# Up projection of the second layer's feed-forward part: two float32 products per tile against six float32r products of split operands

## What is computed

```
n  = layernorm(x3_in) * ln_gamma + ln_beta             # (4096, 256)
W1 = (fc1_q - 128) * fc1_scales                        # (256, 1024), scale per 128 rows
h  = silu(n @ W1 + fc1_bias)                           # the up projection
y  = h @ W2 + fc2_bias                                 # W2 likewise; down projection
```

## Time and profile before

| what | value |
|---|---|
| time, median of 3 runs | 1133.39 us (1132.06 to 1133.58) |
| the profiled execution's own time | 1132.27 us |
| its span, first to last instruction | 1130.5 us |
| mean granted PE clock over the span | 0.967 of full |
| busy: PE, PEld | 1023.1 us (91%), 701.0 us (62%) |
| busy: DVE, ACT, POOL | 922.9 us (82%), 841.1 us (74%), 701.5 us (62%) |
| chain that ended last, by engine | PE 18%, ACT 9%, DVE 8%, issue 5%, POOL 3% |
| up projection on PE, 7 blocks (L40 bank_m<-oa,w) | 103.2 us in 224 MATMULs |

### The profile page before, as it was taken

The page is one execution under the profiler, slowest core; times in us unless marked ns, Lnnn a source line. Parts: engine busy times, 40 slices in busy tenths (PEclk is TensorE's granted clock), DMA queues, the critical chain, the costliest instruction groups (busy, mean ns, idle before and its releaser), DMA issues. The chain is left out here.

```text
span 1130.5 us, 17117 instructions
## 1 busy us (share of the span) xinstructions
PE 1023.1 (91%) x5234; PEld 701.0 (62%) x5234; DVE 922.9 (82%) x1166; ACT 841.1 (74%) x1641; POOL 701.5 (62%) x623
## 2 busy tenths in 40 slices
PE   5999999999969999998758699999999999988987
PEld 4777777777744344444536367567676766767576
DVE  7899999999843566545899998999999899999741
ACT  7778877887644455556767888898998989896843
POOL 2466666766751444435766968869697886968420
PEclk9999999999989999999778899999999999999999
DMA  6344434442404011114976576557566675755201
GB/s 195 113 131 129 129 99 136 121 134 82 137 26 163 1 37 38 38 53 102 240 152 165 127 166 131 151 131 172 139 146 167 142 162 139 151 137 133 81 1 37
DMA packets 93230, 133.81 MB, mean 118 GB/s; under 512 B 8786, under 2 KB 47698, under 8 KB 93140
## 3 DMA queue, kind: packets, MB, share of 16 engines
q1 hardware_dynamic: 93140, 132.73, 44.5%
HBM read 116.45 MB, written 14.16 MB: 116 GB/s over the span
## 5 line engine op out<-in xcount | busy, mean ns | idle before, releaser
L2219 DVE TENSOR_TENSOR_SCAN oa<-bank_a,h,oa 128x512 f32<-128x512 f32 x128 | 159.7, 1270 | 13.7 <-ACT h L1896 10.8
L2219 DVE TENSOR_TENSOR_SCAN ob<-bank_a,h,ob 128x512 f32<-128x512 f32 x128 | 160.5, 1269 | 9.4 <-ACT bank_a L1887 7.0
L1714 PE MATMUL bank_m<-w,f_h 128*128 128x256 f32 x448 | 104.7, 384 | 0.0
L40 PE MATMUL bank_m<-oa,w 128*128 128x512 f32 x224 | 103.2, 595 | 1.2 <-ACT oa L1954 0.9
L1887 ACT ACTIVATE bank_a<-dtc,A 128x512 f32<-128x512 f32 x128 | 86.7, 683 | 16.0 <-DVE oa L2219 8.6
L1887 ACT ACTIVATE bank_a<-s,A 128x512 f32<-128x512 f32 x128 | 86.4, 682 | 15.3 <-DVE oa L2219 9.2
L1714 PEld LDWEIGHTS bank_m<-w,f_h 128*128 128x128 f32 x448 | 84.8, 193 | 13.1 <-issue 2.4
L1669 PE MATMUL bank_y<-ident,ob 128*128 128x128 f32 x512 | 71.5, 286 | 19.9 <-DVE ob L2225 19.9
L1892 ACT ACTIVATE bank_c<-Cb 128x512 f32<-128x512 f32 x128 | 75.5, 590 | 17.3 <-DVE ob L2225 13.2
L2428 POOL TENSOR_TENSOR oa<-uc,Bb 128x1024 f32<-128x1024 f32 x32 | 75.7, 2366 | 20.4 <-DVE ob L2225 13.4
L1669 PEld LDWEIGHTS bank_y<-ident,ob 128*128 128x128 f32 x512 | 63.0, 148 | 39.7 <-DVE ob L2225 22.6
(11 more groups left out here) (374 smaller groups left out, 2735.0 us busy)
## 6 DMA issues: line engine op xcount, KB each, us to landing
Bb<-CB_rows SPq DMA_DIRECT2D x128, 256.0 KB, 5.0
Cb<-CB_rows SPq DMA_DIRECT2D x128, 256.0 KB, 4.6
abc<-decays SPq DMA_DIRECT2D x32, 512.0 KB, 4.4
Ebc<-ramps SPq DMA_DIRECT2D x64, 128.0 KB, 3.0
uT<-in_uT SPq DMA_DIRECT2D x8, 512.0 KB, 4.6
u<-in_u SPq DMA_DIRECT2D x8, 512.0 KB, 3.9
x_tokens<-x2s SPq DMA_DIRECT2D x8, 512.0 KB, 2.9
x_rows<-x1T SPq DMA_DIRECT2D x8, 512.0 KB, 2.8
```

The lines of the kernel that those rows point to most:

```text
L40: i = e.matmul(out, w, x, start=(n == 0), stop=(n == len(pairs) - 1))
L1714: i = e.matmul(to, f_h[:, k, c * CH:(c + 1) * CH], w2[:, k, :], start=False, stop=(c % 2 == 1 and k == KF - 1))
L2219: e.tensor_tensor_scan(s[:, k, :], p_a[k][:, :], s[:, k, :], h0[:, n, k:k + 1], ALU.mult, ALU.add).then_inc(v_s, 1)
```

## The change

- `w1` becomes two float32r tiles, `w1_h` (rounded) and `w1_l` (the remainder). The integer codes are loaded into two tiles that are idle then; `weights(6)` makes the float32 product in place of `s1`, `weights(8)` rounds it, and a new `weights(15)` subtracts.
- `evac_normed` reads its PSUM bank twice on ACT: once into `nT_h` (float32r), once into `nT` (float32) as before. `end_normed` likewise, in halves.
- POOL makes `nT_l = nT - nT_h` in `low_normed`, between `into 13` and `drive`; in the last block DVE does so in `end_low`.
- `up_proj` and `end_up` sum six float32r passes, and the first of each block waits for the remainder.
- The semaphores of constants in the first layer are merged (`a_W`, `a_negA`, `a_id`, `a_rate` into `a_const`; `v_init`, `v_negA`, `v_W` into `v_const`; `p_Wo` into `p_const`), and `v_q` into `v_m`, with counts adapted; the order of instructions stays.

```diff
-        w1, w2 = sb("w1", [P, KD, FF]), sb("w2", [P, KF, DM])
+        w1_h, w1_l = (sb(n, [P, KD, FF], F32R) for n in ("w1_h", "w1_l"))
+        w2 = sb("w2", [P, KF, DM])
...
-            loaded += [(w1[:, :, :].bitcast(I32), rows(d["f_q1"])), (w2[:, :, :].bitcast(I32), rows(d["f_q2"]))]
+            q1 = [flat(dtc[0]).bitcast(I32), flat(uc[0]).bitcast(I32)]
+            loaded += [(q1[k], rows(d["f_q1"])[:, k, :]) for k in range(KD)] + [(w2[:, :, :].bitcast(I32), rows(d["f_q2"]))]
...
                     if w == 6:
                         e.wait_ge(ld, DMAS * len(loaded))
-                        e.tensor_scalar(w1[:, :, :], w1[:, :, :].bitcast(I32), -128.0, None, ALU.add).then_inc(c_w, 1)
+                        for k in range(KD):
+                            e.scalar_tensor_tensor(s1[:, k, :], q1[k], -128.0, s1[:, k, :], ALU.add, ALU.mult).then_inc(c_w, 1)
...
-                        e.tensor_tensor(w1[:, :, :], w1[:, :, :], s1, ALU.mult).then_inc(c_w, 1)
+                        e.tensor_copy(w1_h[:, :, :], s1).then_inc(c_w, 1)
...
+                    if w == 15:
+                        e.wait_ge(c_w, 5)
+                        e.tensor_tensor(w1_l[:, :, :], s1, w1_h[:, :, :].bitcast(F32), ALU.subtract).then_inc(c_w, 1)
...
                 def up_proj(b, m):
                     if m == 0:
-                        e.wait_ge(a_ft, 2 * b + 2)
+                        e.wait_ge(a_ft, 4 * b + 4)
+                        e.wait_ge(p_nl, b + 1)
                     elif m > 1:
                         e.wait_ge(a_up, 8 * b + m - 1)
-                    passes(e, pair[m % 2][:, :], [(w1[:, k, m * P:(m + 1) * P], nT[:, k, :]) for k in range(KD)]).then_inc(pe_up, 1)
+                    ws = slice(m * P, (m + 1) * P)
+                    passes(e, pair[m % 2][:, :], [(w[:, k, ws], x[:, k, :]) for w, x in ((w1_h, nT_h), (w1_l, nT_h), (w1_h, nT_l)) for k in range(KD)]).then_inc(pe_up, 1)
...
                 def end_up(p, m):
                     if m == 0:
-                        e.wait_ge(a_ft, 2 * Z + 2 * p + 2)
+                        e.wait_ge(a_ft, 4 * Z + 4 * p + 4)
+                        e.wait_ge(v_nl, p + 1)
...
                 def evac_normed(b, k):
                     after(e, pe_up, 8 * b)
                     e.wait_ge(pe_ft, 2 * b + k + 1)
+                    e.activation(nT_h[:, k, :], pair[k][:, :], ACT.Identity, bias=lb[:, k:k + 1], scale=lg[:, k:k + 1]).then_inc(a_ft, 1)
                     e.activation(nT[:, k, :], pair[k][:, :], ACT.Identity, bias=lb[:, k:k + 1], scale=lg[:, k:k + 1]).then_inc(a_ft, 1)
...
                     for k in range(KD):
-                        e.activation(nT[:, k, p * DM:(p + 1) * DM], wide[p][:, k * DM:(k + 1) * DM], ACT.Identity, bias=lb[:, k:k + 1], scale=lg[:, k:k + 1]).then_inc(a_ft, 1)
+                        for to in (nT_h, nT):
+                            e.activation(to[:, k, p * DM:(p + 1) * DM], wide[p][:, k * DM:(k + 1) * DM], ACT.Identity, bias=lb[:, k:k + 1], scale=lg[:, k:k + 1]).then_inc(a_ft, 1)
...
+                def end_low(p):
+                    ts = slice(p * DM, (p + 1) * DM)
+                    e.wait_ge(a_ft, 4 * Z + 4 * p + 4)
+                    e.tensor_tensor(nT_l[:, :, ts], nT[:, :, ts], nT_h[:, :, ts].bitcast(F32), ALU.subtract).then_inc(v_nl, 1)
...
                 second(Y, 1)
+                end_low(0)
                 stats6(Y, 1)
+                end_low(1)
...
+                def low_normed(b):
+                    e.wait_ge(a_ft, 4 * b + 4)
+                    e.sem_inc(step, 1)
+                    e.tensor_tensor(nT_l[:, :, :], nT[:, :, :], nT_h[:, :, :].bitcast(F32), ALU.subtract).then_inc(p_nl, 1)
...
                         into(cur, 13)
+                    if 0 <= post < NB - 1:
+                        low_normed(post)
                     if live(nxt):
                         drive(nxt)
```

More of the change, by code:

```diff
@@ L150, in first_layer @@
             ld_W = [sem(f"ld_W{part}") for part in range(3)]
-            p_const, p_Wo, a_W, a_negA, a_id, v_init, v_negA, v_W, a_rate = (sem(n) for n in (
-                "consts", "W_out", "W_h", "expA", "diag", "zeroed", "negA", "W_l", "rates"))
+            p_const, a_const, v_const = (sem(n) for n in ("consts", "a_consts", "v_consts"))
             early = [(cn_w1, rows(d["cn_w1"])), (cn_w2, rows(d["cn_w2"])),
@@ L297, in carried @@
                     e.wait_ge(a_Dx, g + 1)
-                    e.wait_ge(v_init, 4)
+                    e.wait_ge(v_const, 4)
                     after(e, a_S, g)
@@ L518, in split_W @@
                     e.wait_ge(ld_W[part], DMAS)
-                    e.activation(W_h[:, :, W_part[part]], W_in[:, :, W_part[part]], ACT.Copy).then_inc(a_W, 1)
+                    e.activation(W_h[:, :, W_part[part]], W_in[:, :, W_part[part]], ACT.Copy).then_inc(a_const, 1)
                 e.wait_ge(ld_col, DMAS)
                 e.preload_act_table_set(EXP_LN)
-                e.activation(negA[:, :], vec_at["A_log"], ACT.Exp).then_inc(a_negA, 1)
+                e.activation(negA[:, :], vec_at["A_log"], ACT.Exp).then_inc(a_const, 1)
                 e.wait_ge(p_const, 6)
@@ L526, in scalar @@
                     i = e.activation(b_id[:, c * CH:(c + 1) * CH], ident[:, :], ACT.Copy)
-                i.then_inc(a_id, 1)
-                e.wait_ge(v_init, 4)
+                i.then_inc(a_const, 1)
+                e.wait_ge(v_const, 4)
                 split_u(0)
@@ L614, in scalar @@
                     if it == 2:
-                        e.activation(A[:, :, :].rearrange("p k n -> p (k n)"), vec_at["c_A_log"], ACT.Exp).then_inc(a_rate, 1)
+                        e.activation(A[:, :, :].rearrange("p k n -> p (k n)"), vec_at["c_A_log"], ACT.Exp).then_inc(a_const, 1)
                     if live(old):
@@ L717, in low_W @@
                 def low_W(part):
-                    e.wait_ge(a_W, part + 1)
-                    e.tensor_tensor(W_l[:, :, W_part[part]], W_in[:, :, W_part[part]], W_h[:, :, W_part[part]].bitcast(F32), ALU.subtract).then_inc(v_W, 1)
+                    e.wait_ge(a_const, part + 3)
+                    e.tensor_tensor(W_l[:, :, W_part[part]], W_in[:, :, W_part[part]], W_h[:, :, W_part[part]].bitcast(F32), ALU.subtract).then_inc(v_const, 1)
                 def first_low_u():
@@ L746, in net_columns @@
                     e.tensor_scalar(hg3[:, :], gc_b3, 0.5, None, ALU.mult)
-                    e.wait_ge(a_rate, 1)
+                    e.wait_ge(a_const, 6)
                     e.tensor_scalar(A[:, :, :], A[:, :, :], -1.0, None, ALU.mult)
-                e.memset(raw[:, :, TB:TB + TAPS - 1], 0.0).then_inc(v_init, 1)
-                e.memset(S[:, :, :], 0.0).then_inc(v_init, 1)
-                e.memset(Sb[:, :, :], 0.0).then_inc(v_init, 1)
-                e.memset(zeros[:, :], 0.0).then_inc(v_init, 1)
-                e.wait_ge(a_negA, 1)
-                e.tensor_scalar(negA[:, :], negA[:, :], -1.0, None, ALU.mult).then_inc(v_negA, 1)
+                e.memset(raw[:, :, TB:TB + TAPS - 1], 0.0).then_inc(v_const, 1)
+                e.memset(S[:, :, :], 0.0).then_inc(v_const, 1)
+                e.memset(Sb[:, :, :], 0.0).then_inc(v_const, 1)
+                e.memset(zeros[:, :], 0.0).then_inc(v_const, 1)
+                e.wait_ge(a_const, 1)
+                e.tensor_scalar(negA[:, :], negA[:, :], -1.0, None, ALU.mult).then_inc(v_const, 1)
                 first_low_u()
@@ L1166, in z_first @@
                 def z_first(p):
-                    e.wait_ge(c_w, 11)
+                    e.wait_ge(c_w, 12)
                     e.wait_ge(c_xT, 11 + p)
@@ L1480, in build @@
             xl, xn, x3, x3b = (t(n, [P, NC, DM])[:, :, :] for n in ("xl", "xn", "x3", "x3b"))
-            f_h = t("f_h", [P, KF, TB])
+            f_h, nT_h = t("f_h", [P, KF, TB]), t("nT_h", [P, KD, TB], F32R)
+            nT_l = t("nT_l", [P, KD, TB], F32R)
             state, prod, gT, nT = [oa[0], ob[0], oa[1], ob[1]], [ob[2], oa[2]], ob[3], oa[3]
@@ L1500, in build @@
             turned, wide, up_at = p_a, (p_c, p_m[1]), (p_y[0], p_y[1], p_a[0], p_a[1])
-            v_e, v_b, v_m, v_q = (d_sem("v_" + n) for n in ("e", "b", "m", "q"))
+            v_e, v_b, v_m = (d_sem("v_" + n) for n in ("e", "b", "m"))
+            p_nl, v_nl = d_sem("p_nl"), d_sem("v_nl")
             half = slice(0, 2), slice(2, 4)
@@ L1749, in end_up @@
                         e.wait_ge(a_up, 8 * Z + (m | 1) + 1)
-                    ts = slice(p * DM, (p + 1) * DM)
-                    passes(e, up_at[m // 2][:, (m % 2) * DM:(m % 2 + 1) * DM], [(w1[:, k, m * P:(m + 1) * P], nT[:, k, ts]) for k in range(KD)]).then_inc(pe_up, 1)
+                    ts, ws = slice(p * DM, (p + 1) * DM), slice(m * P, (m + 1) * P)
+                    passes(e, up_at[m // 2][:, (m % 2) * DM:(m % 2 + 1) * DM], [(w[:, k, ws], x[:, k, ts]) for w, x in ((w1_h, nT_h), (w1_l, nT_h), (w1_h, nT_l)) for k in range(KD)]).then_inc(pe_up, 1)
                 def end_down(p):
```

32 lines of the change are left out of this document (16 added, 16 removed).

## The result

The changed kernel takes 1153.38 us (median of 4 runs, 1152.76 to 1154.67), the kernel before 1133.49 us in the 4 runs beside it: ratio 1.0181, with a 95% interval from 1.0165 to 1.0196. The change costs 20 us. The prediction was 1147 us, 14 more than before, with a range from 1135 to 1159.

The account below looks back on a forecast made before the run. It took a loop of DVE and ACT to set the scan stage's pace, with PE following with slack, and PE to be the path at the end. 13.0 + 1.2 + 0.4 = 14.6 us more gave 1147 us, range 1135 to 1159.

Parts of the forecast that it names:

- part 4: Last block's halves: more evacuations and end_low delay PE, 48 short passes at 0.125 us apart; 1.2 us more (0 to 11.5).
- Rival (a): Scan stage: PE sets the pace, so 15 us come back and the kernel gets faster, 1118 us; chance 10%.
- rival (b): Scan stage: ACT and DVE regain the 1.7 us in the silu burst; about +2, 1135 us; chance 7%.
- Part 1: Up projection in the scan stage: PE saves 2.1 us per block, 15 in seven, worth 0 to the kernel.
- Part 2: Two more evacuations on ACT per block in the scan stage: the instructions themselves cost 0.1 us.
- Part 3: Scan stage: POOL's remainder delays up_proj(0), then ACT, then scan(13, 0); 1.70 us per block, 13.0 in all (0 to 20).
- Part 5: Making the split weights, mainly the subtraction in weights(15), costs 0.4 us (0 to 1); merged semaphores cost 0.
- (c): Last block: short passes are bound by weight loads, 11.5 us instead of 1.2; 1157 us; chance 10%.
- (d): Scan stage: POOL's added 2.37 us operation holds up a DVE scan, 17 us on top; 1164 us; chance 4%.

Follow-up runs that it names:

- short wait: Changed kernel with add_up 10 ahead of up_proj(0), the remainder made in halves, and only the last two passes waiting, each for its half: 1138.09 us, 1.0054.
- filled float32 kernel: Changed kernel with float32 up_proj products in seven blocks, no weights' remainder, and ten identity products on PE ahead of the wait: 1155.75 us, 1.0209.
- instructions alone: Kernel before plus the second evacuation on ACT and the remainder on POOL, unread, in seven blocks; PE stays float32 and never waits for POOL: 1135.47 us, 1.0026.
- end-only: Kernel before with float32r passes in the last block alone, ordered so that the remainder is hidden: 1129.88 us against 1131.76, 0.9978.
- filled kernel: Changed kernel with twelve needless identity products on PE in each of the last block's two waits for the remainder: 1151.60 us, 1.0182.
- moved evacuation: Changed kernel with evac_up(0) moved on ACT behind carry 11, decay(13, 0) and spread_C 12: 1151.04 us, 1.0158.
- float32 products: Changed kernel with up_proj of seven blocks multiplying float32 nT by rounded weights, all waits kept: 1167.05 us, 1.0297.
- late wait: Changed kernel with up_proj(0) waiting for POOL's remainder only before its fifth pass: 1143.17 us, 1.0087.

## Why the prediction was right, and where it was short

The time lies in the range, and the chain that was forecast for the scan stage is in the trace and answers to edits of its links. The size was short, 14.6 us against 20.6, and the term that was most wrong is part 4.

**What bounds the kernel.** Right. With the wait short and PE's products shorter, the block is not shorter (67.18 against 66.98), so PE does not set the pace; that DVE and ACT do is read from the waits. Rival (a) falls with that, and rival (b) with the trace: nothing took the wait back.

**Part 1, PE's time is worth 0.** Right for the kernel before and for the short wait. Too simple for the change itself, where PE is late: there 2.1 us of products are worth 0.85 per block, by the filled float32 kernel. The sum did not suffer, since it had let the 2.1 us only make PE catch up. The passes came as priced, 0.232 to 0.235 apart.

**Part 2** gave 0.1 us per block; the instructions alone cost a steady block 0.24, POOL's among them.

**Part 3, the wait.** Right in every link, each a little short. PE waits 2.43 us for POOL (2.5 predicted), ACT 2.65 (2.5), DVE 1.69 (1.6), and the remainder ends 3.85 us after the old `nT` (3.7). Offsets from the gate of the fourth block:

| us | before | after | later by | predicted |
|---|---|---|---|---|
| up_proj(0) starts | 47.26 | 50.51 | 3.25 | 3.1 |
| evac_up(0) starts | 49.17 | 52.19 | 3.02 | 2.83 |
| decay(13, 0) starts | 50.68 | 52.87 | 2.19 | 2.02 |
| scan(13, 0) starts | 51.73 | 53.68 | 1.95 | 1.70 |

The 0.25 are small handoffs: POOL starts 0.18 us behind ACT's end (786.89 to 787.07), PE 0.15 behind POOL's, and the scan 0.81 behind the start of its decay, where I had taken 0.1, 0.1 and 0.73.

In the second block the reading was wrong, though the number (4.0 against 2.8) looks near. The 0.97 us of slack that I missed there did not cost anything: the wait before scan(13, 0) is 1.69 us as in every block. In its place DVE waits 3.46 us for `bank_c` where it had waited 1.21. The kernel with the instructions alone, which has no new wait, shows 3.49 us there; the end-only kernel, whose code in that block is that of before, shows 2.79 and took 65.82 us against 64.25. In all three ACT waits 2.8 to 2.9 us for the transposes at evac_normed(0), just ahead of spread_C 10, where it had waited 1.27, and the stretch of half clock in which they run is 10.2 us long instead of 6.8. So of the 4.0 us 1.7 are the named wait, about 0.7 the second evacuation ahead of spread_C 10 (I had taken 0.1), and about 1.6 a stretch of half clock that end-only has without any change in this block; what makes it longer stays open. The last block varies by as much: end-only took 68.55 there against 67.07. In the changed kernel PE's wait there was 4.60 us and was followed by half clock, for which the 1.7 had no term; its 2.3 can't be told from scatter.

And the prediction followed the lateness through evac_up(0) alone; moving that one showed evac_up(1) as the next that hands it on.

**Part 4, the end.** Here the prediction failed by most of its error: 4.9 us against 1.2. The two waits are as predicted (1.72 and 1.69 more, 1.7 named). The passes are 0.119 apart at full clock where I took 0.125, so 48 take 5.8 us and not 6.1; and the 32 MATMULs of before took 7.0 and 6.8 us, not 7.2, since their transposes take 0.6 us of the distance and not 0.44. The two errors cancel. The page TensorE: Matmul & The Clock Gate of the Trainium skill (section Back-to-back issue gap) has a formula for the gap of an isolated MATMUL, by which the estimate was 0.109; the trace lies between, nearer to mine, and decides. What failed is that I priced the passes at full clock behind a wait that the change itself makes. At half clock they are (1114.67 - 1113.39) / 6 = 0.213 apart. The estimate by that section's formula for the low clock, columns / 1.2 ns, is 0.213 too. The first half took 7.28 us instead of 5.8 and the second 7.09. That is 2.8 of the missing 3.7 us, by the filled kernel.

The rest is 1.15 us at the out projection. The gate came earlier against the rest, since PE had caught up: DVE waited for the last sum 1.64 us instead of the 2.79 of the earlier trace rows. But ACT's normalization beside it did not. It now waits for POOL's `nb`, which is made from DVE's statistics of `x3b`, and these stand 1.14 us closer to the gate than before. So ACT's copy to `ob` and PE's out projection (its first MATMUL, with the bias, at 1088.77) start 1.15 us later from the gate. ACT's normalization before, and DVE's gate and the same ACT row after:

```profile
1069.24 2.07 ACT L1970 ACTIVATE x3b<-x3b,nb,rs 128x256 f32<-128x256 f32 x4
```
```profile
1085.37 1.29 DVE L2243 TENSOR_TENSOR zgs<-bank_y,zgs 128x512 f32<-128x512 f32 x2 [1.64 <-PE bank_y L1676]
1086.16 2.07 ACT L1981 ACTIVATE x3b<-x3b,nb,rs 128x256 f32<-128x256 f32 x4 [1.04 <-POOL nb L2480]
```

So of the 2.1 us of shorter products that I let come back in the last scan, about half was lost again behind the gate. The filled kernel has the same 1.15 at full clock, so the half clock that happens to stand there (the 3.09 us of the first `w_o` products) cost nothing: the next ones wait for ACT anyway.

**Part 5, the weights.** Predicted 0.4. No run can tell: the first scan of the third stage starts between 535.3 and 537.7 us in the kernels with the new weights, and at 536.6 and 535.5 in the two with the old ones.

**Rivals (c) and (d).** (c) needed 0.232 per short pass; it is 0.119. (d) did not happen: the pair of scans that begins at 788.60, across the end of POOL's remainder, takes 2.45 us as before, and the instructions alone, POOL's among them, cost a steady block only 0.24 us. The rule on ports of the page SBUF — State Buffer (Trainium skill, section Who interferes with whom) agrees.

**The sum.** Predicted 13.0 + 1.2 + 0.4 = 14.6. Measured in the profiled executions, by the table of gates: 17.1 + 4.9 - 1.3 = 20.7 (20.6 as the difference of the spans, by rounding). Of the 6 us missing, 2.8 are the clock in the end, 1.2 the half clock in the fifth block, 1.1 the small excess of the other blocks from the third to the seventh, 1.15 the out projection; the second and the last block hold 1.8 that cannot be told from scatter, the stages before gave 1.7 back, which is scatter too and was luck, and 0.3 came back elsewhere in the end. Fewer busy microseconds on PE were no sign of anything: 10 less (17 predicted), with the half clock taking part of the gain.

## What to carry to other kernels

When a product is replaced by a faster one that needs one more prepared operand, follow the new operand to the first instruction that waits for it, and then every queue behind that instruction: here 2.1 us saved on an engine with slack bought 2 us lost on the engine without it. Order the passes so that those needing the late operand come last, and start preparing it in halves; that alone took back 14 of 20 us. And behind every wait that an edit adds on PE, price the next products at half clock as well as at full, and let the range hold both.

## What the runs showed of the hardware that was not expected

The granted clock behind a wait of PE. Behind 2.90 and 2.80 us of idle time in the end the products ran at half clock for 3.4 us; with identity products in the gap they did not. Without a filling, half clock is likely there but not certain: seven kernels have this end, and 13 of their 14 waits (2.79 to 3.02 us) were followed by half clock; the first one of the kernel with the moved evacuation, 2.90 us, was not. Behind 2.43 us in the scan stage it happened, among the six blocks from the second to the seventh, in one of the changed kernel's execution (the fifth block), in two with the moved evacuation, in four of the filled-end kernel's, with the same code there, and in five with float32 products, all but the second. Waits of 1.36 us (the late wait) and of 1.17 and 1.11 us (end-only) had none behind them in these blocks and ends. The wait and what stands before it are alike in all blocks of a kind, so the trace does not tell which wait will be followed by half clock; what decides it stays open. It also means that such a wait has a price that differs from one block to the next: the fifth block took 70.13 us here and the fourth, with the same work, 68.95.

As the prediction had it, a loaded ACT and POOL mind more work little: two evacuations of 0.66 us and one POOL operation of 2.35 us cost a steady block 0.24 us, with ACT busy 90% of the block before.
